# Selective scan of a ViT tower on one core: ScalarE's copy-back placed ahead of the y eviction, and two decay quads ahead of a read-out on TensorE

## The reference

```python
dA = jnp.exp(delta[..., None] * A)
dBx = delta[..., None] * Bm[:, :, None, :] * x[..., None]

def step(h, inputs):
    dA_t, dBx_t, C_t = inputs
    h = dA_t * h + dBx_t
    y_t = jnp.einsum('bdn,bn->bd', h, C_t)
    return (h, y_t)
```

## Time and profile before

| | us |
|---|---|
| median of 3 runs | 1066.46 (1065.74 to 1068.66) |
| the profiled execution's own time | 1074.73 |
| its span (first to last instruction) | 1072.8 |
| VectorE busy in the span | 667.0 (62%) |
| TensorE matmuls busy | 916.5 (85%) |
| ScalarE busy | 500.6 (47%) |
| the scan, steps 1 to 36 on VectorE | 156.2 to 432.5 |

### The profile page before, as it was taken

One profiled execution on the slowest core, in us unless ns is written; L12 is line 12 of the kernel. 1 busy time (PEld: TensorE's weight loads), 2 busy tenths in 40 slices (PEclk: granted clock), 3 DMA queues, 4 the chain that ended last, 5 costly groups with the idle time before them and its releaser, 6 DMA issues.

```text
span 1072.8 us, 17620 instructions
## 1 busy us (share of the span) xinstructions
PE 916.5 (85%) x5865; PEld 591.1 (55%) x5866; DVE 667.0 (62%) x1146; ACT 500.6 (47%) x946; POOL 289.4 (27%) x357
## 2 busy tenths in 40 slices
PE   8997586788778886898999999999999996479996
PEld 6773443333333332446777777667666764346664
DVE  1543786889999999554544455457767786423332
ACT  1225666888898984243222222334454433223332
POOL 4922602433243131000000000064444430602122
PEclk9997858888999999898999999969999998789999
DMA  6273469554222215831311111000000000823221
GB/s 243 94 257 128 175 200 304 144 155 112 56 45 49 58 39 183 332 157 39 101 46 46 45 56 35 0 1 2 1 2 0 1 2 0 295 74 91 72 86 30
DMA packets 96401, 100.67 MB, mean 94 GB/s; under 512 B 64334, under 2 KB 81615, under 8 KB 94672
## 3 DMA queue, kind: packets, MB, share of 16 engines
q1 hardware_dynamic: 93600, 92.52, 27.2%
q0 software_dynamic: 2736, 7.30, 1.9%
HBM read 73.12 MB, written 39.18 MB: 105 GB/s over the span
## 4 chain that ended last, share of the span: by engine, by line
PE 59%; DVE 15%; issue 12%; ACT 6%; DMA 4%; SPq 2%; POOL 0%; ACTq 0%; DVEq 0%; POOLq 0%
PE ps L567 9%; PE ps L629 8%; DVE mem L2100 6%; PE ps L1564 5%; PE ps L1580 4%; PE ps L1126 4%; PE ps L1456 3%; PE ps L1390 3%; PE ps L1245 2%; DVE mem L2084 2%; PE ps L1412 2%; PE ps L1402 2%; DMA slots<-mem,slot_i 2%; ACT mem L1705 1%; PE ps L1153 1%
## 5 line engine op out<-in xcount | busy, mean ns | idle before, releaser
L1083 POOL TENSOR_TENSOR mem<-mem 128x296 f32<-128x296 f32 x128 | 86.9, 714 | 354.8 <-ACT mem L1800 314.6
L1705 ACT ACTIVATE mem<-ps 128x512 f32<-128x512 f32 x288 | 155.5, 614 | 34.5 <-PE ps L1205 16.3
L1060 POOL TENSOR_SCALAR mem<-mem,sm 128x16 f32<-128x16 f32 x148 | 100.1, 699 | 189.6 <-PE ps L1245 189.6
L1205 PEld LDWEIGHTS ps<-mem 64*128 64x128 bf16 x1140 | 64.4, 101 | 88.9 <-ACT mem L1705 68.6
L567 PE MATMUL ps<-mem 128*128 (+1 forms) x384 | 110.2, 417 | 0.6 <-DVE mem L540 0.6
L1212 PE MATMUL ps<-mem 64*128 64x512 bf16 x296 | 67.1, 413 | 49.1 <-DVE mem L2100 24.1
L629 PE MATMUL ps<-mem 128*128 128x296 f32 x352 | 99.9, 413 | 2.3 <-DVE mem L693 2.3
L1205 PE MATMUL ps<-mem 64*128 64x128 bf16 x1140 | 94.5, 234 | 7.1 <-ACT mem L1705 6.9
L653 ACT ACTIVATE mem<-ps 128x296 f32<-128x296 f32 x88 | 36.7, 418 | 134.9 <-PE ps L567 130.7
L2089 DVE TENSOR_TENSOR ps<-mem 128x1024 f32<-128x1024 f32 x72 | 88.5, 1229 | 15.2 <-ACT mem L1730 15.1
L2084 DVE TENSOR_TENSOR mem<-mem 128x1024 f32<-128x1024 f32 x72 | 88.1, 1224 | 13.6 <-ACT mem L1705 13.6
(11 more groups left out here) (259 smaller groups left out, 1590.5 us busy)
## 6 DMA issues: line engine op xcount, KB each, us to landing
mem<-gates SPq DMA_DIRECT2D x7, 1184.0 KB, 6.1
mem<-in_w SPq DMA_DIRECT2D x2, 4096.0 KB, 16.4
slots<-mem SPq DMA_DIRECT2D x1, 6682.0 KB, 23.7
mem<-slots SPq DMA_DIRECT2D x26, 257.0 KB, 2.6
mem<-in_patches SPq DMA_DIRECT2D x7, 864.0 KB, 4.5
mem<-factor_rows SPq DMA_DIRECT2D x296, 16.0 KB, 1.8
mem<-factor_rows SPq DMA_DIRECT2D x37, 128.0 KB, 2.3
mem<-delta_rows SPq DMA_DIRECT2D x9, 512.0 KB, 4.5
```

The costliest lines, as they stand in the source:

```text
L1060: nc.gpsimd.tensor_scalar(c_win4[:, t % WINS * 2 + r, :, w0:w0 + 8].rearrange("p j (x i) -> p j x i", i=2)[:, :, :, i], c_all[:, r * 16:r ...
L1083: last = nc.gpsimd.tensor_tensor(kbd[p % 2][:, a, im, :, :], bc(kT[cj][:, a, t0:t0 + L], 1, 8), bc(mask, 2, L), ALU.mult)
L1205: mm = nc.tensor.matmul(ps[:, ring_bank(at_), e * BT:(e + 1) * BT], a_stat[64 * r:64 * r + 64, g, e, :], delta_in[b % 2][64 * r:64 * r + 6 ...
L1705: nc.scalar.activation(decay_slots[b % 2][:, :, 4 * k:4 * k + 4], ps[:, ring_bank(at_), :].rearrange("p (e t) -> p t e", e=4), ACT.Exp).th ...
```

## The change

Two places in the streams of TensorE and ScalarE change, in odd steps only. No instruction is added or taken out.

```diff
--- before.py
+++ after.py
@@ -1288,12 +1288,14 @@
                     if m % 2 == 0:
                         if 1 <= t < L:
                             inject(t, m)
-                        next_quads(t, m, first)
+                        opens_pair = m == 2 and t % 2 == 1
+                        next_quads(t, m, all_of if opens_pair else first)
                         if t >= 1 and m == 0:
                             read_state(t - 1, 1)
                         if t < L and m == 2:
                             read_state(t, 0)
-                        next_quads(t, m, rest)
+                        if not opens_pair:
+                            next_quads(t, m, rest)
                     else:
                         if 1 <= t < L:
                             grow(t, m)
@@ -1742,10 +1744,10 @@
             copy_grown(0, 3)
             for t in range(L + 1):
                 for m in range(GROUPS):
+                    if 1 <= t < L and m % 2 == 1:
+                        copy_grown(t, m)
                     if m == 1 and t % 2 == 1:
                         evict_rows(t // 2)
-                    if 1 <= t < L and m % 2 == 1:
-                        copy_grown(t, m)
                     if t < L and m == 3 and t % 2 == 1:
                         copy_y(t // 2)
                     for b, k in quads_made(t, m) if t < L else []:
```

## The result

The changed kernel takes 1084.74 us (median of 4 runs, 1083.61 to 1089.48) against 1067.56 us for the kernel before (4 runs, 1065.74 to 1068.95). The ratio is 1.0162, with a 95% interval of 1.012 to 1.0204: 17 us slower. I had forecast slower, by 5.5 us, with a range up to 1078. The direction was right, the size was three times too small.

The account below looks back on a forecast made before the run. VectorE was taken as the bound. Terms 2.9 (full clock), 3.4 (half-clock block starts) and 0.2 (steps 33 and 35) sum to 6.5 us, taken as 5.5 on the median 1066.46: 1072.0 us, range 1067.0 to 1078.0.

Parts of the forecast that it names:

- VectorE is the bound, and its waits are what can change: In the scan: VectorE is busy 27.49 to 27.58 us per block, so the change acts only through its idle time.
- Full clock: 0.36 us per block, the moved quad behind a pushed Exp: Block start and third step: later eviction and Exps delay quad, read-out and `grow`; 8 blocks x 0.36 = 2.9 us.
- A: Rival: ScalarE's holes swallow the lag, block-start waits stay 1.49, time 1066.5 us; chance 0.20 together with another rival.
- Block start at half clock: 0.48 more, in seven starts: Behind block starts at clock 0.50: later read-out delays the seed, 0.48 us beyond the 0.36, seven times, 3.4 us.
- The bound of 1.8 us per block: Block starts: if the half-clock stretch lasts longer, one block costs up to 30.76 - 28.98 = 1.8 us more.
- Third steps stay at full clock: Third step of each block: TensorE's clock assumed to stay at 1.00, so no half-clock cost there in the sum.
- Rival C: Third steps: TensorE's hole of about 0.8 us halves the clock, 0.65 per block, 5.2 more, 1077.2 us; chance 0.12.
- Steps 33 and 35: 0.2: Late steps without quads: the read-out waits for the later eviction; VectorE may lose 0.1 us each, 0.2 in all.
- Rival B: Block starts: half-clock stretches move or vanish, 7.1 us go and 3.1 come, 1062.5 us; chance 0.10.
- The step to the median: Whole run: the median may have fewer half-clock stretches than the profiled execution, so 5.5 us taken instead of 6.5.

Follow-up runs that it names:

- e6: Changed kernel plus five repeated injections at block starts and three between the m = 2 quads of odd steps; 1066.47 us, ratio 0.9973 to before.
- e5: Kernel before, with the injection of m = 0 repeated five times at block starts; 1062.73 us, ratio 0.9938 to the kernel before.
- e9: Kernel before with only ScalarE's part of the change, plus the repeats of e6; 1063.05 us, ratio 0.9951 to the kernel before.
- e10: Kernel before with only TensorE's part of the change, plus the repeats of e6; 1064.19 us, ratio 0.9952 to the kernel before.
- e4: Kernel before with both parts of the change, but only in third steps (t = 3, 7, 11, ...); 1076.42 us, ratio 1.0072 to before.
- e11: As e5, plus 22 repeats of the second quad's four matmuls in the long hole of step 1; 1063.49 us, ratio 0.9954 to before.
- e1: Kernel before with only ScalarE's part of the change, TensorE's order as before; 1074.71 us, ratio 1.0071 to the kernel before.

## Why the prediction was wrong

*VectorE is the bound, and its waits are what can change*: right. Its busy time stayed within 0.3 us per block, so nearly all of the 16.2 us in the scan is waiting. The sum had 6.5 us for the profiled execution: 2.9 at full clock, 3.4 for block starts at half clock, 0.2 for the last steps. Measured were 3.2, 12.0 and 1.0.

*Full clock: 0.36 us per block, the moved quad behind a pushed Exp*: right in mechanism and nearly in size. e6 against e5 gives 29.37 - 28.93 = 0.44 (means of the first six blocks). Over seven blocks it is 205.63 - 202.44 = 3.2 us; steps 1 to 4, which I had counted as an eighth, lost nothing. ScalarE at a block start of e6:

```profile
314.54 1.03 ACT L1756 ACTIVATE mem<-ps 128x1024 f32<-128x1024 f32 x1 [1.83 <-PE ps L1212]
315.46 0.59 ACT L1740 ACTIVATE mem<-ps 128x512 f32<-128x512 f32 x1
315.94 2.08 ACT L1731 ACTIVATE mem<-ps 128x512 f32<-128x512 f32 x4
318.43 1.02 ACT L1756 ACTIVATE mem<-ps 128x1024 f32<-128x1024 f32 x1 [0.42 <-PE ps L1212]
```

Copy to copy is 3.89 us, against 3.40 in the earlier trace rows: +0.49, and I had 0.47. The decays' wait at block starts is 1.59 (I had said 1.7 to 1.8 and A 1.49); the rest is lost in front of seeds, mostly about 0.1 each before the seed of quarter 3 in the second and the fourth step, in waits too short to be listed. At the second of these seeds VectorE is 0.26 us late against the full-clock block of before, where the working had 0.20. That both parts are needed for it (e9, e10) I had not said, though the working has it: the +0.47 enters by the eviction, and reaches `grow` by the quad.

*Block start at half clock: 0.48 more, in seven starts*: this term of the sum failed. Measured against the same order at full clock (e5 and e6), half clock cost 209.94 - 202.44 = 7.5 us in seven blocks before and 225.12 - 205.63 = 19.5 after: 12.0 more instead of 3.4. The third steps, below, make about 4.8 of it, which leaves some 7.2 for the block starts. I priced the start as one read-out that is late and then gets its time back, and the earlier trace rows shows only the first wait behind it. The trace of before already had 0.30 and 0.79 more behind that 0.60. In the changed kernel the seed waits 1.10 to 1.24 instead of 0.6, in three of seven blocks followed by 0.53 and 1.12 to 1.17. The stretch at half clock there is no longer than in the long blocks before (6.8 us in both); what it delays has changed. Over the seven blocks the time at half clock (twice the length of a block times what its mean clock lacks to 1, summed) grew from about 31 to about 45 us, while what it cost went from 7.5 to 19.5. The bound of 1.8 us per block that I named and did not use was the better guide.

*Third steps stay at full clock*, which the sum put at nothing: the other part of the same failure. Rival C was right, to which I gave 0.12: three third steps of seven fall to half clock, for 1.59, 1.58 and 1.65 us of seed waits, 4.8 in all. I priced it at 0.65, from the mildest halved blocks, where the read-out was not in front of `grow`. By the changed order a halved read-out delays `grow` directly. My argument against C, that a hole of 1.85 us had once left the clock at 1.00 at 346.51, took one case of seven as the rule. The page of the Trainium skill that I cited, "TensorE: Matmul & The Clock Gate", section "A second HAM failure mode: psum-queue depth-cycling", spoke for C, and the traces of the changed kernel and of e4 agree: idle spells of about 0.85 us between quads, and read-outs of 1.93 instead of 1.06. But the same hole is followed by the full clock in the four other third steps of the changed kernel, so it does not say when the clock falls.

*Steps 33 and 35: 0.2*: measured 1.0. VectorE waits 0.53 and 0.30 for copies in the steps after 33 and 35, and TensorE's mean clock there is 0.82 instead of 0.94. In e6 this stretch is at 1.00 and takes 27.35 us, as before, so this loss too is the clock's.

*Rival B, the half-clock stretches may go*: wrong for this change, right as an idea. With the holes filled (e5) the 7.5 us come back.

*The step to the median*: I took 1.0 off the sum, thinking that the median run has fewer half-clock stretches. That may hold for the kernel before: its profiled execution has a mean clock of 0.923, its runs of 1066.1 to 1066.8 us taken along with e9 to e11 one of 0.929 to 0.931. It did not hold for the changed kernel. Its four runs lie at 1083.61 to 1089.48 with clocks of 0.915 to 0.921, the profiled one being the lowest. There is no trace of a run of the kernel before near its median, so where its 8.3 us lie is not shown.

What stays open: why the blocks of so many variants settle at 30.6 to 31.1 us (e1 to e4 and before in its first three), why every third block of the changed kernel is 33.9 long, and why the same hole is followed by half clock in one block and by full clock in the next. The runs show that the lengths are tied to the clock, since they are gone where the clock is held, but none varies the length of a block by itself.

## What to carry to other kernels

Ask of every moved wait on TensorE not only who waits behind it but what the hole does to its clock: the same read-out takes 1.06 or 1.93 us, and the cost is paid by whatever the other engines wait for behind it. Where a short stretch of a trace runs at half clock without loss, put the next thing on the path behind it only if it can bear the doubled time. Repeating a harmless matmul in a hole, with the semaphore on the last one, tests in one run whether the clock is the cause, and may be the gain itself (here 0.6%).

## What the hardware showed that I had not expected

TensorE can be busy without a gap and stay at half clock: in e11 the 89 matmuls that the trace shows in the hole kept it busy for 9.7 us at a granted clock of 0.50, where it had been before them. Five repeats of two injections per block, about 1.1 us of work in 28.9, held it at 1.00 in all seven blocks of e5. A change of 0.44 us per block at full clock became 2.2 us per block through the clock. And the price of a half-clock stretch is set by what stands behind it: in steps of the same kind, block starts, 0.2 to 1.7 us before and 1.5 to 2.9 after.
